# Four attention blocks on one core: a projection copied once from its PSUM bank, and layer norm in single pieces between the row maxima

## What is computed

```python
def _layernorm(x, axis=-1, eps=1e-05):
    m = jnp.mean(x, axis=axis, keepdims=True)
    v = jnp.var(x, axis=axis, keepdims=True)
    return (x - m) / jnp.sqrt(v + eps)
...
    # the split block, shortened
    q_n = q_pure / jnp.linalg.norm(q_pure, axis=-1, keepdims=True)
    sim = (qg_n[None, None] * q_n).sum(-1).mean(-1)
    sim = (sim - sim.min()) / (sim.max() - sim.min())
    pos = sim > 0.9
...
    x = L0_attn_a_x
    x = x + attn_a(_layernorm(x))   # causal
    x = x + ffn(_layernorm(x))      # split
    x = x + attn_b(_layernorm(x))   # rotary
    x = x + ffn(_layernorm(x))      # split
```

## Time and profile before

| what | us |
|---|---|
| median of 3 runs | 4944.91 (4940.63 to 4948.76) |
| the profiled execution, its own time | 4945.49 |
| its span in the trace | 4943.7 |
| PE busy in the span | 4445.3 |
| DVE busy | 3209.4 |
| ACT busy | 2548.2 |
| POOL busy | 1656.7 |

### The profile page before, as it was taken

How to read it: one execution, slowest core, us unless ns; L and a number is a source line. 1 busy time by engine, 2 the same in 40 slices (tenths; PEclk the granted TensorE clock), 3 DMA queues, 4 the chain that set the end, 5 groups by cost and what they waited for, 6 DMA issues and landing times.

```text
span 4943.7 us, 70632 instructions
## 1 busy us (share of the span) xinstructions
PE 4445.3 (90%) x26116; PEld 1877.8 (38%) x26116; DVE 3209.4 (65%) x6576; ACT 2548.2 (52%) x3362; POOL 1656.7 (34%) x922
## 2 busy tenths in 40 slices
PE   4899999999969999899898999999999699999998
PEld 2454545454423333333333333333333233333333
DVE  4555555555447776767676676676676277777776
ACT  1444444444425555555455555555555255666565
POOL 2354545454432344352534334334324400000000
PEclk8999999999979999999999999999999799999999
DMA  4453535344322333423333334334333133333331
GB/s 131 122 155 118 156 114 156 124 150 127 107 89 82 92 114 96 114 83 113 99 96 112 98 113 120 96 106 120 98 104 120 54 86 90 89 89 90 91 89 44
DMA packets 302406, 525.36 MB, mean 106 GB/s; under 512 B 58348, under 2 KB 236272, under 8 KB 285680
## 3 DMA queue, kind: packets, MB, share of 16 engines
q1 hardware_dynamic: 259568, 485.19, 33.7%
q10 hardware_dynamic: 42496, 35.66, 2.2%
HBM read 317.10 MB, written 201.46 MB: 105 GB/s over the span
## 4 chain that ended last, share of the span: by engine, by line
PE 71%; DVE 17%; DMA 6%; issue 3%; ACT 3%; POOL 1%; DVEq 0%; ACTq 0%; SPq 0%; POOLq 0%
PE o_ps L1249 17%; PE scores L1197 16%; PE scores_t L1228 11%; DVE neg_max L864 10%; PE turn_ps L1277 10%; DMA q_stack<-shift_rows 5%; PE turn_ps L1324 5%; PE turn_ps L1284 4%; PE turn_ps L1255 4%; DVE bn L822 2%; DVE xn L839 2%; PE turn_ps L1289 1%; DVE shift_parts L874 1%; PE scores L1200 1%; PE scores L1212 1%
## 5 line engine op out<-in xcount | busy, mean ns | idle before, releaser
L864 DVE TENSOR_REDUCE neg_max<-scores 128x1 f32<-128x512 f32 (+3 forms) x4096 | 2489.2, 636 | 1285.9 <-PE scores L1197 760.0
L1065 ACT ACTIVATE probs<-scores_t 128x1024 f32<-128x1024 f32 (+2 forms) x2048 | 1926.3, 947 | 1484.8 <-PE scores_t L1228 1007.3
L1197 PE MATMUL scores<-k_stack,q_stack 98*128 98x512 bf16 (+4 forms) x4096 | 1428.3, 371 | 239.6 <-DVE neg_max L864 179.5
L1228 PE MATMUL scores_t<-q_stack,k_stack 100*128 100x512 bf16 (+3 forms) x4096 | 1187.5, 364 | 59.2 <-DMA q_stack<-shift_rows 58.3
L1249 PE MATMUL o_ps<-probs,values 128*32 128x512 f32 (+1 forms) x8192 | 1021.4, 571 | 0.2 <-ACT probs L1065 0.2
L1197 PEld LDWEIGHTS scores<-k_stack,q_stack 96*128 96x128 bf16 (+1 forms) x4096 | 396.7, 97 | 1635.8 <-DVE neg_max L864 1209.1
L1228 PEld LDWEIGHTS scores_t<-q_stack,k_stack 100*128 100x128 bf16 x4096 | 378.4, 99 | 380.5 <-issue 137.7
L725 POOL TENSOR_TENSOR parts<-qk_f,parts 128x1024 bf16<-128x1024 f32 x128 | 272.6, 2130 | 660.3 <-ACT parts L1105 491.1
L745 POOL TENSOR_TENSOR sim_inv<-sim_parts,minus_half 128x64 f32<-128x64 f32 x32 | 337.7, 10552 | 249.9 <-DVE sim_parts L946 249.9
L738 POOL TENSOR_TENSOR x_res<-x_res,o_bias_s 128x1024 f32<-128x1024 f32 x32 | 75.6, 2362 | 956.8 <-DMA x_res<-x_after 956.8
L696 POOL TENSOR_SCALAR var_eps<-mean_var 128x4 f32<-128x4 f32 x64 | 14.7, 230 | 978.6 <-DVE mean_var L828 978.6
(11 more groups left out here) (117 smaller groups left out, 4035.2 us busy)
## 6 DMA issues: line engine op xcount, KB each, us to landing
q_stack<-q_parts SPq DMA_DIRECT2D x1536, 64.0 KB, 2.6
values<-v_stage SPq DMA_DIRECT2D x64, 1024.0 KB, 4.2
values<-values SPq DMA_DIRECT2D x64, 1024.0 KB, 6.2
k_parts<-parts SPq DMA_DIRECT2D x192, 256.0 KB, 2.7
q_parts<-parts SPq DMA_DIRECT2D x192, 256.0 KB, 3.3
k_stack<-k_parts SPq DMA_DIRECT2D x256, 192.0 KB, 3.2
k_stack<-k_parts SPq DMA_DIRECT2D x256, 128.0 KB, 3.2
x_after<-x_res ACTq DMA_DIRECT2D x48, 512.0 KB, 2.9
```

Source lines behind the costliest of these rows:

```text
L864: nc.vector.tensor_reduce(neg_max[:, h % G, t:t + 1], bank[:, 0:n], AX.X, ALU.max, negate=True).then_inc(max_done.sem, 1)
L1065: nc.scalar.activation(probs[c][:, h % G, 0:n], st[i][:, 0:n], ACT.Exp).then_inc(exp_done.sem, 1)
L1197: last = nc.tensor.matmul(bank[:, 0:n], q[0:r, h, t * P:(t + 1) * P], k[0:r, h, 0:n], start=True, stop=kind != CAUSAL)
L1228: last = nc.tensor.matmul(st[i][:, off:off + L - q0], k[0:ROWS, h, kt * P:(kt + 1) * P], q[0:ROWS, h, q0:L], start=True, stop=kind != CAUSAL)
```

## The change

ScalarE reads the bank once in a `qk` or `nq` turn, and that copy alone counts up `turn_free`. The high part and the square are then made from the copy in SBUF, behind a wait for it; the last of them counts up a new semaphore `projected`, for which POOL's `prepare` and the `sim` turn on PE wait. For a rotary next stage there was only the one copy and stays so. The layer norm is cut into pieces of one tile each: four `bn_stats`, one group of four `bn_aggr`, four normalisations, each behind one maximum, by tables that give a piece for a slot and a maximum. DVE turns stay behind maxima 1 and 3.

```diff
-NXT_STATS_AT = (6, 1)
-NXT_NORMALISE_AT = (8, 0)
-X_STATS_AT = (8, 1)
-X_NORMALISE_AT = (10, 1)
+NXT_STATS_AT = {(6, 0): 0, (6, 2): 1, (6, 3): 2, (7, 0): 3, (7, 1): T}
+NXT_NORMALISE_AT = {(8, t): t for t in range(T)}
+X_STATS_AT = {(9, 0): 0, (9, 1): 1, (9, 2): 2, (9, 3): 3, (10, 0): T}
+X_NORMALISE_AT = {(11, t): t for t in range(T)}
...
+        projected = Count(sem("projected"), steps_of(
...
-                turn_free.wait(pool, B, FRONT[f][1], a + 1)
+                if kind_of(B, f) == ROTARY:
+                    turn_free.wait(pool, B, FRONT[f][1], a + 1)
+                else:
+                    projected.wait(pool, B, FRONT[f][1], a + 1)
...
+            def statistics(B, f, piece):
+                x = x_new if f == OWN else x_res
+                if piece < T:
+                    if f == NXT:
+                        dve.wait_ge(turn_free.sem, turn_free.after(B, "out", piece // 2))
+                    elif piece == 0:
+                        dve.wait_ge(x_loaded.sem, x_loaded.after(B, f))
+                    last = nc.vector.bn_stats(bn[:, piece, :], x[:, piece, :])
+                    if piece == T - 1:
+                        last.then_inc(bn_done.sem, 1)
                 else:
-                    dve.wait_ge(turn_free.sem, turn_free.after(B, "out", 1))
+                    xn_done.wait_earlier(dve, B, 1, f)
+                    dve.wait_ge(bn_done.sem, bn_done.after(B, f))
+                    for t in range(T):
+                        last = nc.vector.bn_aggr(mean_var[:, t, :], bn[:, t, :])
+                    last.then_inc(stats_done.sem, 1)
+
+            def normalise(B, f, t):
+                if t == 0:
+                    dve.wait_ge(rstd_done.sem, rstd_done.after(B, f))
...
                 x = x_new if f == OWN else x_res
+                last = nc.vector.tensor_scalar(xn[:, t, :], x[:, t, :], mean_var[:, t, 0:1],
+                                               rstd[:, t:t + 1], ALU.subtract, ALU.mult)
+                if t == T - 1:
+                    last.then_inc(xn_done.sem, 1)
...
                     scale = DH ** -0.5 if i < 2 else 1.0
                     if kind == CAUSAL:
                         bias = q_bias[:, i:i + 1] if i < 2 else qk_bias[:, i:i + 1]
-                        project = lambda dst: nc.scalar.activation(dst, turn_ps[:, :], ACT.Identity, bias=bias, scale=scale)
+                        nc.scalar.activation(qk_f[:, i, :], turn_ps[:, :], ACT.Identity, bias=bias,
+                                             scale=scale).then_inc(turn_free.sem, 1)
                     else:
-                        project = lambda dst: nc.scalar.activation(dst, turn_ps[:, :], ACT.Copy, scale=scale)
-                    last = project(qk_f[:, i, :])
+                        nc.scalar.activation(qk_f[:, i, :], turn_ps[:, :], ACT.Copy, scale=scale).then_inc(turn_free.sem, 1)
                     if kind != ROTARY:
-                        last = project(parts[:, i, 0, :])
-                    if kind == SPLIT and i < 2:
-                        last = nc.scalar.activation(q_square[:, i, :], turn_ps[:, :], ACT.Square, scale=scale)
-                    last.then_inc(turn_free.sem, 1)
+
+                        act.wait_ge(turn_free.sem, turn_free.after(B, k, i))
+                        last = nc.scalar.copy(parts[:, i, 0, :], qk_f[:, i, :])
+                        if kind == SPLIT and i < 2:
+                            last = nc.scalar.activation(q_square[:, i, :], qk_f[:, i, :], ACT.Square)
+                        last.then_inc(projected.sem, 1)
...
+                elif k == "sim":
+                    pe.wait_ge(projected.sem, projected.after(B, "nq", 1))
```

More of the change, by code:

```diff
@@ new lines, in normalise @@
+            def normalise(B, f, t):
+                if t == 0:
+                    dve.wait_ge(rstd_done.sem, rstd_done.after(B, f))
+                    before, key = front_before(B, f)
+                    if before is not None:
+                        turn_full.wait(dve, before, key, 1)
+                x = x_new if f == OWN else x_res
+                last = nc.vector.tensor_scalar(xn[:, t, :], x[:, t, :], mean_var[:, t, 0:1],
+                                               rstd[:, t:t + 1], ALU.subtract, ALU.mult)
+                if t == T - 1:
+                    last.then_inc(xn_done.sem, 1)
@@ L843, in register_queries, with layer_norm @@
+            def layer_norm(B, f):
+                for piece in range(T + 1):
+                    statistics(B, f, piece)
+                for t in range(T):
+                    normalise(B, f, t)
             def register_queries(B):
@@ L992, in first @@
                     for b in range(X_AHEAD):
-                        statistics(B + b, OWN)
-                        normalise(B + b, OWN)
+                        layer_norm(B + b, OWN)
                         if b < OWN_AHEAD:
@@ L1010, in body, with normal @@
                 kind = STAGES[B.s]
-                def normal(slot, place):
-                    here = (slot, place)
+                def normal(slot, t):
+                    here = (slot, t)
                     if there(B.s, B.n - 1) and has_next((B + (-1)).s):
[L1015 to L1018, removed]
+                        if here in NXT_STATS_AT:
+                            statistics(B + (-1), NXT, NXT_STATS_AT[here])
+                        if here in NXT_NORMALISE_AT:
+                            normalise(B + (-1), NXT, NXT_NORMALISE_AT[here])
@@ L1019, in normal @@
                     if B.s == 0 and B.n + X_AHEAD < NB:
[L1020 to L1023, removed]
+                        if here in X_STATS_AT:
+                            statistics(B + X_AHEAD, OWN, X_STATS_AT[here])
+                        if here in X_NORMALISE_AT:
+                            normalise(B + X_AHEAD, OWN, X_NORMALISE_AT[here])
@@ L1025, in body @@
                 for slot in range(H):
                     m = max_head(B.s, B.n, slot)
[L1027 to L1030, removed]
+                    for t in range(T):
+                        if t == T - 1 and kind == SPLIT and slot == EXTRA_AT:
                             extra_max(B)
                         if m:
-                            maximum(B + m[0], m[1], 2 * place + 1)
-                        if place and m and m[1] % G == G - 1:
+                            maximum(B + m[0], m[1], t)
+                        if t == T - 1 and m and m[1] % G == G - 1:
@@ L1035, in body @@
                             shift(B + m[0], m[1] // G)
[L1036 to L1039, removed]
+                        if t % 2:
+                            for k, off, i in turns_of(B.s, B.n, slot, t // 2):
+                                if k in DVE_TURNS:
+                                    take_turn(B + off, k, i)
@@ L1040, in body @@
+                        normal(slot, t)
                 if there(B.s, B.n + 1):
@@ L1047, in finish @@
                     if (k, i) == ("out", 1) and has_next(B.s):
-                        statistics(B, NXT)
-                        normalise(B, NXT)
+                        layer_norm(B, NXT)
             run(dve, first, body, finish)
```

15 lines of the change are left out of this document (5 added, 10 removed).

## The result

The changed kernel took 4795.24 us (median of 4 runs, 4788.87 to 4806.5) against 4946.84 beside it on the same chip: ratio 0.9695, interval 0.9668 to 0.9722. The profiled execution took 4788.9, its span is 4787.1.

The account below looks back on a forecast made before the run. PE was taken as the bound, an edit being worth what it takes from PE's idle time. Pieces 60 plus bank 57 made 117 us; less some 10, 107 us saved: 4838 us, own range 4815 to 4860.

Parts of the forecast that it names:

- (a): Rival: gaps only move, since DVE and the shift DMA bound slots 7 and 8; 71 us saved, 4874; chance 0.2.
- (d): Rival: slower, as each piece delays a maximum; 5021 us if all delays reach PE; chance 0.05.
- the late shift DMA: Stage 2, first tile of slot 8: a shift DMA taking 3.7 us pushes maximum 0 by 0.45 us.
- NXT pieces, stage 2: Slot 7's 1.22 us PE gap goes; replay puts `nx` 0.86 us earlier, 0.5 taken; 15 bodies, 7.5 us.
- NXT pieces, stage 1: Slot 7's 1.53 us gap: replay puts the `nx` turn 1.6 us earlier, 1.5 taken; 16 bodies, 24 us.
- NXT pieces, stage 0: 0.96 us gap behind the NXT statistics: `nx` waits for the last piece, gaining 0.85 us in 15 bodies.
- OWN pieces, stage 0: Gaps of 0.69 and 0.49 us behind OWN statistics and normalisation both go, in 13 bodies.
- bank, stage 2: Gaps of 0.80 and 0.31 us behind query and key turns both go; 15 x 1.11 = 16.7 us.
- bank, stage 0: Gaps behind query and key turns, the last `qk` turn's transposes and `qk` copies go; 37 us.
- The cover of ACT: ACT's 1.20 us idle ahead of a turn covers 192 copies each 0.15 us later; 29 us if it failed.
- (c): Rival: POOL holds OWN normalisation pieces 2 and 3 in slot 11, losing 55 us; 4893; chance 0.05.
- (e): Rival: PE's earlier start pulls DVE, POOL and the next shift DMAs along; up to 140 us saved, 4805; chance 0.07.

Follow-up runs that it names:

- norm_only: Kernel before the change with only the layer norm cut into pieces, ScalarE reading the bank up to three times as before; 4869.27 us, ratio 0.9848.
- act_only: Kernel before the change with only ScalarE's single read of the bank, layer norm left in blocks; 4874.92 us, ratio 0.9863.
- hold_bank: Kernel before, layer norm in blocks, high part and square made from the SBUF copy, but the bank freed only by the last; 4969.73 us, ratio 1.0051.
- x_at_13: Changed kernel with the four OWN normalisation pieces in slot 13 in place of 11, beside GpSimd's parts; 4822.84 us, ratio 0.9745.

## Why the prediction was wrong in size and right in kind

The gaps that the forecast named closed, at their places, and none of (a) to (d) set the time. But the late shift DMA that it counted on in stage 2 did not come, and every term of the sum but that of stage 1 was too small. Measured by medians over the bodies of the distances between turns on PE (before less after; norm_only and act_only show the same differences to 0.1):

```
                          per body: predicted, measured   sum: predicted, measured
NXT pieces, stage 2                    0.5       1.16           7.5      17
NXT pieces, stage 1                    1.5       1.57          24        25
NXT pieces, stage 0                    0.85      1.33          13        20
OWN pieces, stage 0                    1.18      1.47          15        19
bank, stage 2                          1.11      1.45          17        22
bank, stage 0                          2.47      2.97          37        40
bank, start and stage ends                                      3         8
taken off                                                     -10         0
sum                                                           107       151
```

(The 2.97 holds for the 12 bodies that also carry stage 0's own projections; the last three gain 1.3 to 2.2 us, so the sum of 40 is taken from the table of columns, 1162.0 less 1121.8. The measured 8 is what is left of the 151; the profiled pair has 14 us at the start and between stages.)

Of the 44 us that the sum was short of, some 15 come from pricing waits by their gap rows, 10 from the replay of stage 2 and its DMA, 10 from the deduction, 5 from the start and the stage ends, and most of the rest from the replay of stage 0. The failed steps, in the prediction's words:

- **"idle for 0.80 us, and 0.31 us behind the key turn ... Both gaps go: 15 x 1.11".** The failed step is to take a gap row as the whole cost of a wait. The two went, and gave 0.95 and 0.47. In stage 0 the turns of 0.39 and 0.88 us of gap gave 0.49 and 1.03, and one between two query turns that has no gap in its row gave 0.15. The two gaps behind OWN, 0.69 and 0.49, gave 0.86 and 0.66. So these waits cost 0.10 to 0.17 us more than their rows, and a wait shorter than that has no row; only behind stage 0's own `qk` turns was the shortfall small, 0.06 and 0.01. This is most of the 8 us missing from the bank in the bodies and the 4 missing from OWN.
- **"this tile can start at 3318.8 ... pushes maximum 0 of slot 8 by 0.45 us ... I take 0.5".** Wrong in stage 2: it bounded the landing of a DMA by 3.7 us from the end of a body, while the tile of slot 8 started, without waiting, 2.55 us after the issue. The packet records of the trace before, which no view lists one by one, already told the two apart: the last packet of the transfer issued at 3315.16 ended 1.54 us after the issue, that of the one issued at 824.36 after 3.26 us. Of the 15 that were issued in slot 6 in stage 2, 14 took 1.51 to 1.54 us and one 2.50.
- **"That ends at 3323.1 ... 0.86 us".** Without the DMA the replay was the better figure, but the first `nx` turn came 1.22 us earlier (0.05 is lost again behind it, which leaves the 1.16). DVE needed 7.68 us from the start of piece 2 (3184.10) to the end of the last normalisation (3191.78), where the replay had 8.04. It took 0.38 us for the aggregation, its length, though the next operation started 0.29 us behind it, and 0.62 for a maximum, though eight maxima between other work followed at 0.59 to 0.60.
- **"For NXT the `nx` turn again waits for the last piece: replayed, it gains 0.85 of the 0.96".** In stage 0 it gained 1.33: 1.13 where the gap row had 0.96, and 0.19 in the stretch behind it, up to `nx`. The mechanism held, for `nx` starts 0.06 us behind the end of the last piece (969.22 and 969.16 in one body). That the wait cost 0.17 more than its row explains a part; which step of the replay missed the rest stays open, since the prediction shows only its result.
- **Stage 1** was right to 0.1 us. Its replay moved the `nx` turn by 1.6 us, from 2019.93 to 2018.3, and by the medians it moved by 1.61. Since the same replay was 0.36 short in stage 2, part of this hit may be luck.
- **"I take off some 10 for a piece or exponential that comes late".** Nothing came late enough: inside the bodies of stages 0 and 2 no PE turn waits for `parts` or `x_both` any more, and of the 46 us of the earlier trace rows 9.3 are left, now behind the first copy, in 24 cases of at most 0.8.
- **The cover of ACT** held, and its price was well placed: copy and square took 618 and 624 ns, 27 and 21 more than from the bank, and with the wait the exponential came 0.24 us later behind a query turn (1.69 us after the turn's first operation, 1.45 before). That hold_bank lost 27 us, near the 29 given as the price of a failed cover, is chance: there PE waits for the bank, the exponentials are still covered, and no run here shows what an uncovered one costs. The Trainium skill (VectorE: DVE Perf Modes, the TRN2 errata) gives 43 ns more from SBUF. The runs lie on both sides of it: the durations differ by 27 and 21 ns, the distances from one start to the next by 48 and 54 (525 and 531 ns from SBUF, 477 from the bank), and it is the distance that the following operation feels. For stage 0's own projections the later copy became shorter, 618 ns where it had been 680 from the bank with a bias.
- **(c) was argued away wrongly.** The mechanism is real; only its place was wrong. The step "the 406 ns speak against it" took the speed of an operation as evidence on what it locks. In the changed kernel the pieces of slot 11 end before GpSimd's parts begin (980.7 and 982.75 in one body), so there was nothing to hold. The one normalisation that does meet a GpSimd tensor operation took 1.41 us:

```profile
156.84 2.35 POOL L752 TENSOR_TENSOR x_res<-x_res,o_bias_c 128x1024 f32<-128x1024 f32 x1
157.94 1.41 DVE L854 TENSOR_SCALAR xn<-x_new,mean_var,rstd 128x256 f32<-128x256 f32 x1
```

x_at_13 put the OWN pieces beside such operations and lost 28 us, half of the 55 priced, and a part of that through the shift operations pushed along. The price had counted two pieces a body at 2.1 us each, all felt by PE; three were held, and DVE has idle time in slot 13. The Trainium skill (VectorE: DVE Perf Modes, the perf-mode tier table, and SBUF — State Buffer, two separate sides) was right against the prediction on this.
- **(e)** named an earlier PE that pulls the rest along as the cause of more, at 140 us. The time lay nearer to it than to the forecast, but not for that reason: each gain stayed at its own turns, and between the two edits there was no such pull beyond the 10 us that the intervals leave open.
- **The start** gave 7 us in the profiled pair, and kernels with ScalarE's edit have the first body at 192 to 200 against 202 to 208 for those without. The cause was not taken apart: these kernels also scatter by 4 there.

## What to carry to other kernels

Price a wait by the distance between the starts of two instructions that are the same in a body with the wait and in one without it, not by the idle time in its row; over the short waits of these bodies the difference made some 15 us. In a replay of one engine's list, step from start to start and not by durations. Take the latency of a small DMA from the transfer at the place in question, or from others that nobody waited for, and not only from those that ended a wait. Before moving a normalisation or another SBUF operation on VectorE, look at what GpSimd does at its new place: whether they meet decides between 0.4 and 2 us, the operation's own duration elsewhere tells nothing of it, and what comes behind it may be pushed into the same trouble.

## What the runs showed of the hardware

- A float32 `tensor_scalar` on VectorE of 256 columns takes 0.40 us alone and ends 0.15 us behind GpSimd's tensor operation when it starts beside one (1.08, 2.00 and 1.82 us above). A cast and a subtraction of 16 columns, 0.17 us alone, are held as well (1.45 and 2.27 us). `tensor_reduce` from PSUM beside the same operations is not held, nor was `bn_stats` (four in 1.40 us from 60.87 in the changed kernel, with GpSimd busy from 59.36 to 61.48).
- ScalarE copies 512 float32 columns to bf16 from SBUF in 618 ns and from PSUM in 591. The next operation starts 0.53 us after one from SBUF and 0.48 us after one from PSUM; the f32 copy from PSUM is followed after 0.49 us, and after 0.63 us where the next one waits for it.
- A shift DMA of 8 KB was there for the tile of slot 8 within 2.55 us of its issue (its last packet ended after 1.54 us), while the 73 tiles of the changed kernel that waited for one started 1.99 to 5.1 us after its issue, the longest for the one issued at 2262.6.
